# Linear attention with a mixture of experts on one core: key path ahead of the queries, ε of the keys as a column, and a VectorE add that waits for GpSimd's sums

## The reference

```python
def softmax_kernel(x, proj, is_query):            # per head, x: [.., n, 16]
    xp = einsum('bhnd,md->bhnm', x * norm, proj)
    diag = sum(square(x), -1) * 0.5 * norm * norm
    stab = max(xp, -1) if is_query else max(xp, (-1, -2))
    return ratio * (exp(xp - diag - stab) + EPS_K)
qp, kp = softmax_kernel(q, proj, True), softmax_kernel(k, proj, False)
k_sum = sum(kp, axis=2)
denom = einsum('bhnm,bhm->bhn', qp, k_sum)
ctx = einsum('bhnm,bhnd->bhmd', kp, v)
out = einsum('bhnm,bhmd->bhnd', qp, ctx) / denom[..., None]
x = layer_norm(video + out @ Wo.T + bo); x = layer_norm(x + relu(x @ W1.T + b1) @ W2.T + b2)
...
# experts: scores = softmax(xf @ gate_w.T); top 512 tokens of each expert; two products with gelu; scatter-add
```

## Time and profile before

| | |
|---|---|
| median of 3 runs | 785.98 us (785.49 to 787.17) |
| the profiled execution | 786.12 us |
| its span, first to last instruction | 784.4 us |
| granted TensorE clock, mean | 0.977 |
| PE, PEld busy | 93%, 76% |
| DVE, ACT, POOL busy | 79%, 60%, 48% |
| one turn of the steady loop | 58.1 us |
| end of turn 7 on PE | at 465.6 us |

### The profile page before, as it was taken

The page is one execution under the profiler, slowest core; times in us unless marked ns, Lnnn a source line. Parts: engine busy times, 40 slices in busy tenths (PEclk is TensorE's granted clock), DMA queues, the critical chain, the costliest instruction groups (busy, mean ns, idle before and its releaser), DMA issues. The chain is left out here.

```text
span 784.4 us, 16225 instructions
## 1 busy us (share of the span) xinstructions
PE 728.6 (93%) x6009; PEld 597.0 (76%) x6009; DVE 619.0 (79%) x1304; ACT 469.6 (60%) x749; POOL 375.3 (48%) x358
## 2 busy tenths in 40 slices
PE   8999999999999999999999979968999999999950
PEld 7867768778778778778778758857888889998850
DVE  5976678888888888888888797888768767778683
ACT  4656747867867867867868834463245544455470
POOL 4364317527527527527617613511347556544563
PEclk9999999999999999999999999999999999999985
DMA  8100010011011011011011011250336664446593
GB/s 252 33 2 2 1 54 2 28 54 57 28 53 54 27 53 54 27 53 54 27 54 29 29 55 54 60 193 2 124 134 163 160 165 112 107 148 168 138 266 112
DMA packets 51184, 62.60 MB, mean 80 GB/s; under 512 B 9408, under 2 KB 44992, under 8 KB 51136
## 3 DMA queue, kind: packets, MB, share of 16 engines
q1 hardware_dynamic: 44016, 49.74, 19.3%
q0 software_dynamic: 6864, 12.19, 7.9%
q10 hardware_dynamic: 256, 0.03, 0.0%
HBM read 40.85 MB, written 21.10 MB: 79 GB/s over the span
## 5 line engine op out<-in xcount | busy, mean ns | idle before, releaser
L2181 PE MATMUL pF<-w,h 128*128 128x256 f32 x448 | 109.8, 386 | 0.0
L2181 PEld LDWEIGHTS pF<-w,h 128*128 128x128 f32 x448 | 80.7, 190 | 17.6 <-issue 8.6
L1139 POOL DMA_INDIRECT kp<-row_scratch,idx_g x32 | 43.3, 1353 | 76.5 <-DVE idx_g L1851 53.5
L904 ACT ACTIVATE h<-pX,b1cur 128x512 f32<-128x512 f32 x64 | 43.9, 689 | 56.4 <-DVE b1cur L1954 41.8
L2636 PE MATMUL pX<-w_lo,h_hi 128*128 128x256 f32 x256 | 73.9, 289 | 0.8 <-issue 0.8
L2636 PE MATMUL pX<-w_hi,h_lo 128*128 128x256 f32 x256 | 72.4, 283 | 0.0
L2636 PE MATMUL pX<-w_hi,h_hi 128*128 128x256 f32 x256 | 72.4, 283 | 0.0
L993 POOL TENSOR_SCALAR ve<-mv 128x4 f32<-128x4 f32 x36 | 8.5, 237 | 133.2 <-DVE mv L1216 132.3
L1147 POOL DMA_INDIRECT acc_scratch<-qp,idx_s x28 | 55.5, 1982 | 21.5 <-DVE qp L1891 16.6
L1912 DVE TENSOR_TENSOR h_lo<-h,h_hi 128x512 fp32r<-128x512 f32 x64 | 42.5, 690 | 22.9 <-ACT h_hi L896 22.2
L1321 DVE RECIPROCAL den<-den 128x512 f32<-128x512 f32 x14 | 46.9, 3348 | 7.9 <-ACT den L551 7.9
(11 more groups left out here) (435 smaller groups left out, 2165.6 us busy)
## 6 DMA issues: line engine op xcount, KB each, us to landing
kp<-fc1T SPq DMA_DIRECT2D x8, 1024.0 KB
w<-fc2T SPq DMA_DIRECT2D x8, 1024.0 KB
xin<-video SPq DMA_DIRECT2D x7, 512.0 KB, 3.5
x<-video SPq DMA_DIRECT2D x7, 512.0 KB, 4.5
out<-x SPq DMA_DIRECT2D x7, 512.0 KB, 3.0
acc_scratch<-xf SPq DMA_DIRECT2D x7, 512.0 KB, 2.9
row_scratch<-y SPq DMA_DIRECT2D x7, 512.0 KB, 3.0
kp<-acc_scratch SPq DMA_DIRECT2D x4, 512.0 KB, 5.8
```

Of the source, the lines that this page charges most:

```text
L904: nc.scalar.activation(h[:, n, :], pM[n % M_SLOTS], ACT.Gelu_apprx_tanh, bias=b1cur[:, n:n + 1]).then_inc(he_ready, 1)
L1139: pool.indirect_dma_start(xg[:, g, :], None, row_d, bass.IndirectOffsetOnAxis(ap=idx_g[:, g:g + 1], axis=0)).then_inc(first_rows[g] if isi ...
L2181: ins = nc.tensor.matmul(pF[m][:, half * D:(half + 1) * D], h[:, k, tok(2 * m + half)], w2[:, k, :], start=(k == 0), stop=(k == FC - 1))
```

## The change

1. **ε of the keys.** `eps_k` goes. The key tiles lie with a pitch of 130 instead of 128 columns in a wider tile whose columns 128 and 129 hold ε; `context` reads 129 columns, so its last column is ε times the sum of the values, which `cs_copy(i, 0)` copies to `vsum` and adds as a bias; `cs_copy(i, 1)` adds 512 ε. The first turn's extra matmuls with ε, in `context` and `sums_of_keys`, and GpSimd's two adds for them go too.
2. **TensorE's order** in a turn: `key_features(0)` ahead of `values`; `turn_kmax` behind `hidden(2)` instead of `hidden(5)`; `context` ahead of `features_turned(0)` and without the product between them; `sums_of_keys`, `features_turned(1)` and `turn_context` one behind the other; 16 products of `ff_out` behind `all_heads`, where 10 stood. `spread_kmax` stands alone and reads 128 rows (the rows beyond 16 are zeros).
3. **VectorE's order:** `k_max` 0 and 1 ahead of `x2T_lo`; `q_max` 0 and 1 behind `k_top`; `rest_of_squares` behind `k_sub` 1; `residual` behind `ln1_stats` and `scores`, and it waits for `ksum_ready`.
4. **GpSimd's order:** the sums wait for all four `k_sub`; the add of `bo_b` to `xn` (`biased_rows`) waits for `obias_ready` and stands behind the sums.
5. **ScalarE's order:** `exp_k` 0 and 1 between the last `relu`; `z_norm` behind `exp_k`; `normed_rows` last. SyncE stores the scores of batch u one turn later.

The core of the diff:

```diff
@@ ScalarE, GpSimd @@
-                nc.scalar.activation(cs[:, n, :], pA[n][:, 0:G * P], ACT.Copy).then_inc(cs_ready, 1)
+                if n:
+                    nc.scalar.activation(cs[:, 1, :], pA[1][:, 0:G * P], ACT.Identity, bias=epsn_c[:, 0:1]).then_inc(cs_ready, 1)
+                else:
+                    wide = pA[0][:, 0:G * PW].rearrange("p (g x) -> p g x", x=PW)
+                    nc.scalar.activation(vsum[:].unsqueeze(2), wide[:, :, P:P + 1], ACT.Copy).then_inc(vsum_ready, 1)
+                    act.wait_ge(vsum_ready, i + 1)
+                    for g in range(G):
+                        ins = nc.scalar.activation(cs[:, 0, g * P:(g + 1) * P], wide[:, g, 0:P], ACT.Identity, bias=vsum[:, g:g + 1])
+                    ins.then_inc(cs_ready, 1)
...
-            def eps_k(i, t):
-                act.wait_ge(ke_ready, (i - 1) * TT + t + 1)
-                nc.scalar.activation(kp[:, t, :], kp[:, t, :], ACT.Identity, bias=epsk_c[:, 0:1]).then_inc(kp_ready, 1)
...
+                    pool.wait_ge(ks_ready, (i + 1) * TT)
+                    for t in range(1, TT):
                         pool.wait_ge(kp_ready, i * TT + t + 1)
...
+                if not is_first(i):
+                    pool.wait_ge(obias_ready, i + 1)
+                    biased_rows()
@@ VectorE @@
-                    q_max(i, 0)
-                    q_max(i, 1)
-                    k_top(i, sa)
-                    rest_of_squares(i)
-                    dve.wait_ge(dg_ready, (i + 1) * 2)
-                    k_shift(i)
-                    k_sub(i, 0)
-                    k_sub(i, 1)
-                    q_max(i, 2)
...
+                k_top(i, sa)
+                q_max(i, 0)
+                q_max(i, 1)
+                dve.wait_ge(dg_ready, (i + 1) * 2)
+                k_shift(i)
+                k_sub(i, 0)
+                k_sub(i, 1)
+                rest_of_squares(i)
+                q_max(i, 2)
...
+                if u is not None:
+                    dve.wait_ge(ksum_ready, (i + 1) * (TT - 1))
+                    residual(u, su)
@@ TensorE @@
-                steps = [(v[:, t], kp[:, t]) for t in range(TT)] + ([(vsum[:, 0:D], None)] if is_first(i) else [])
...
+                                ins = nc.tensor.matmul(s[32 * q:32 * q + 32, g * PW:g * PW + P + 1], v[:, t, 32 * pair:32 * pair + 32],
+                                                       kpe[:, t, place_of(pair), 0:P + 1], start=(t == 0), stop=(t == TT - 1),
+                                                       tile_position=(0, 32 * q))
...
+                hidden(2)
+                turn_kmax()
+                hidden(3)
+                hidden(4)
+                spread_kmax()
+                hidden(5)
+                features(i, J_XQ + 1, qT, 1)
+                hidden(6)
+                hidden(7)
+                ff_out(2)
+                turn_tops()
+                ff_out(6)
+                context()
+                features_turned(0)
+                ff_out(4)
+                sums_of_keys()
+                features_turned(1)
+                turn_context()
+                ff_out(4)
+                all_heads()
+                ff_out(5)
```

More of the change, by code:

```diff
@@ L736, in body @@
+                if not is_ahead(i):
                     squares(i, 0)
                     squares(i, 1)
[L738 to L766, removed]
+                key_rows(1)
+                relu(f, 0)
+                relu(f, 1)
@@ new lines, in body @@
+                q_squares(i)
+                for n in range(2, 6):
+                    relu(f, n)
+                exp_k(i, 0)
+                relu(f, 6)
+                exp_k(i, 1)
+                relu(f, 7)
+                q_tops(i)
+                exp_k(i, 2)
+                exp_k(i, 3)
+                if ut:
+                    for t in range(TT):
+                        z_norm(u, t)
+                cs_copy(i, 0)
+                exp_q(i, 0)
+                cs_copy(i, 1)
+                exp_q(i, 1)
@@ L2172, in hidden, with ff_out @@
                     by_halves(slot_f(f, J_H + n), w1_hi, w1_lo, x2T_hi, x2T_lo, n).then_inc(f_ready, 1)
-                def ff_out(m, half, k0=0, k1=FC):
-                    if half == 0:
-                        slot_f(f, J_Y + m)
-                    for k in range(k0, k1):
+                products = [(m, half, k) for m in range(2) for half in range(2) for k in range(FC)]
+                def ff_out(count):
+                    for m, half, k in products[:count]:
+                        if half == k == 0:
+                            slot_f(f, J_Y + m)
                         if m == half == 0:
@@ L2182, in ff_out @@
                                                start=(k == 0), stop=(k == FC - 1))
-                    if half == 1 and k1 == FC:
-                        ins.then_inc(f_ready, 1)
+                        if half == 1 and k == FC - 1:
+                            ins.then_inc(f_ready, 1)
+                    del products[:count]
                 def by_heads(j, w_, g):
@@ L2437, in body @@
-                if att:
-                    features(i, J_XQ + 1, qT, 1)
-                    spread_kmax()
-                if ff:
-                    hidden(7)
-                if ff:
-                    ff_out(0, 0)
-                    ff_out(0, 1, 0, 2)
-                if att:
-                    turn_tops()
-                if ff:
-                    ff_out(0, 1, 2, FC)
-                if att:
-                    features_turned(0)
-                if ff:
-                    ff_out(1, 0, 0, 1)
@@ L2453, in body @@
[L2453 to L2467 removed]
+                key_features(1)
@@ L2472, in body @@
                         turn_tokens(pXall[:, 2 + c, :], xf, c).then_inc(u_ready, 1)
[L2473 to L2474 removed]
+                ff_out(3)
                 if gt_:
```

247 lines of the change are left out of this document (92 added, 155 removed).

## The result

The changed kernel takes 789.63 us (median of 6, 787.73 to 791.23) against 785.49 us for the kernel before: ratio 1.0048, 95% interval 1.0028 to 1.0067. It is slower, by about what was forecast (790.0), but the trace shows that terms of the sum were wrong and cancelled in part. The profiled execution of the changed kernel took 787.73 us and was the fastest of the six.

A forecast was written before the change was run, and what follows sets the result against it. PE's stream plus any wait on PE was taken to bound the kernel. A full turn costs −0.6 + 0.6 + 1.0 = +1.0; with turns 0, 1 and 7 the sum is +4.2, giving 790.0 us, range 779 to 794.

The forecast's parts named there:

- PE's own stream: PE's work in a steady turn, without waits, falls by about 0.6 us, from 58.1 to 57.5.
- First wait: PE at turn_tops waits 0.6 us a turn: DVE's chain from spread_kmax takes 6.94 us against PE's 6.46.
- Second wait: PE at sums_of_keys waits 1.0 us more a turn: subtractions and POOL's three sums make 9.9 us against PE's 8.9.
- Residual, no cost to PE: Residual behind POOL's sums takes 1.23 us instead of 3.39, hidden by PE's work; without that cover, up to 0.5 a turn.
- Turn 0, −0.9: Four groups of ε products of 0.22 us go from a chain leading to the heads: −0.9 us.
- Turn 1, +1.0: k_max ahead of x2T_lo +0.9, both waits +1.6, waits at and behind attention_out gone −1.2, borders −0.3: together +1.0 us.
- Turn 7, −0.9: Heads come earlier in PE's stream, and DVE's reciprocal chain behind them moves along, except for 0.4: −0.9 us.
- The sum: Turn 0 −0.9, turn 1 +1.0, five full turns +5.0, turn 7 −0.9: +4.2 us, giving 790.0 us.
- the waits don't form: Rival: neither wait at turn_tops nor sums_of_keys appears, only PE's stream counts, −7.0 us or 779.0; chance 0.27, in full or larger part.
- one wait only: Rival: only one of the waits at turn_tops and sums_of_keys costs time, 784 to 787 us; chance 0.10.
- POOL holds VectorE elsewhere: Rival: POOL's root for z or small scores products hold VectorE or the sums, 0.9 us a turn, about 795 us; chance 0.08.
- What would show it: Both waits each turn, steady turn 59.1 us, residual 1.23; wrong if a turn is under 58 or PE's waits under 5 us.

The follow-up runs named there:

- e3: Changed kernel with one more ff_out product ahead of turn_tops and one ahead of sums_of_keys, two fewer behind all_heads; 784.94 us, 0.9975 of the kernel before.
- e10: Changed kernel with rest_of_squares moved behind k_sub 3 instead of ahead of q_max 2; 788.72 us, 1.0023 of the kernel before.
- e12: e6 with one more ff_out product ahead of sums_of_keys and one more ahead of turn_x, both from behind turn_x; 780.13 us, 0.9918 of the kernel before.
- e8: Kernel before with only part 1 of the change (pitch of 130, no eps_k, bias of the copies), old orders; 797.87 us, 1.0142 of the kernel before.
- e9: e8 plus the change's two waits: GpSimd's sums for all four subtractions, the residual, behind the statistics, for the sums; 802.40 us, 1.0184 of the kernel before.
- e6: Changed kernel with the edits of e3 and e4, and in turn 1 k_max(1) behind x2T_lo again; 782.16 us, 0.9941 of the kernel before.
- e4: Changed kernel with VectorE's copy of the gates behind turn 7 put after the third reciprocal and product pair; 787.44 us, 1.0010 of the kernel before.
- e1: Changed kernel run again with nothing altered; 790.37 us, 1.0050 of the kernel before.
- e2: Changed kernel with VectorE's residual no longer waiting for GpSimd's key sums; 794.72 us, 1.0101 of the kernel before.
- e11: e10 plus the gates copy moved as in e4 and, in turn 1, the second k_max behind x2T_lo; 786.46 us, 0.9990 of the kernel before.
- e7: Changed kernel without GpSimd's wait for all four subtractions before its sums; 809.18 us, 1.0288 of the kernel before.

## Why the prediction was right, and where it was not

*The bound.* Right: PE's stream plus waits on PE. e3, e10 and e12 change only orders, and the turn became shorter by the waits that went.

*PE's own stream, −0.6.* Measured −0.80 (58.08 to 57.28, and 57.29 in e12). `attention_out` went from 3.40 to 3.02 (forecast −0.3); 0.4 is left for the borders, where I had 0.3.

*First wait, 0.6.* It is there, 0.40. The chain from `spread_kmax` took 6.94 as summed; PE's pieces took 6.59 for 6.46, and the step from DVE to PE 0.05 for 0.15.

*Second wait, 1.0.* It is there, 0.68. The mis-sized term is the pace of the sums: 2.40 for the first and 2.2 for each behind it, 6.9 us for the 7.35 that I summed from the 4.90 for two in turn 1. That row was undisturbed: VectorE ran nothing beside its two sums (2.39 and 2.37) but the last 0.04 us of one operation. In the changed kernel the same pair takes 4.51, and in e8 and e9, which have the old orders and the new layout of the key tiles, an undisturbed sum in place takes 2.18 to 2.20 too. So the gain came with the layout with its pitch of 130; I had taken the layout to leave the sums as they were. Why it helps is not shown. PE's pieces, which I wrote as 8.9 though they sum to 8.84, took 8.72.

So a full turn costs +0.28 and not +1.0 (+0.50 in turn 2), five of them +1.6 and not +5.0.

*Residual, no cost to PE.* Right in the changed order; e9 shows the cover that I named taken away, at 2.6 us a turn (58.08 to 60.64) where I had written 0.5. The part that I had priced, the masked context, is 0.7 of it. I had not priced the other 1.8: in the old order ScalarE's denominators stand behind `xf`, which needs the statistics behind the residual.

*Turn 0, −0.9.* Measured −1.13. Of this 0.91 lies behind the first `features_turned`, as forecast; the other 0.22 lies ahead of it, where from 32 to 40 us the granted clock was 0.79 and 0.78 in the profile before and 1.00 in the changed one. *Turn 1, +1.0.* Measured +0.38; its waits are the same smaller ones (0.47 and 0.65), and the `k_max` costs 0.65 for the 0.9 I gave it (e6). The wait of 1.03 at `attention_out` is gone, as forecast.

*Turn 7, −0.9.* This is the step that failed: +1.09. I had moved VectorE's reciprocal chain with the heads and not seen that it holds a copy which waits for the gates, which the change puts later. e4 puts that at 2.2 us, and −0.9 + 2.2 = +1.3 is near what was measured.

*The sum.* +4.2 forecast; the marks of the two profiled executions give +1.95, the two spans +1.6, the medians +4.1 and, in e1, +3.45. So that 790.0 came so near is luck twice. Within the turns, five were over by 3.4, turn 1 by 0.6 and turn 0 by 0.2, and turn 7 was under by 2.0, which leaves a forecast of +4.2 for a measured +1.95. The medians then hold about 2 us that the sum had no term for and that the two profiled executions do not show. Behind the last mark, with the same code, the profile of the kernel before has 316.1 us, that of the changed kernel 316.2 and those of the e-runs 316.4 to 318.3. Two stretches with a lower clock make most of this: 1.4 us in the first 8 us behind the mark, where the clock is low for 3.4 us (e1, e4 and e9), and 2.0 us between 81 and 97 us behind it (e2, e3, e6, e8, e10, e11 and e12). At the second place the clock is low for 3.5 us in the two first profiles and for 10.1 in those seven. A window of PE there in e10, then in the changed kernel, 94 us behind the mark in both:

```profile
562.93:564.93 2.00, 2.00 (x9) 0.50 0.60 172
```

```profile
563.78:565.78 2.00, 2.00 (x13) 1.00 0.60 168
```

e8 and e9, with the orders of the kernel before, have such stretches too. The mean granted clock over the executions of e1 was 0.974 for the changed kernel and 0.975 for the kernel before, so whether the changed kernel meets them more often stays open.

*The rivals.* That the waits don't form fell, as they are in every turn; one wait only fell too. That POOL holds VectorE elsewhere did not happen in the changed kernel's steady turns: `sdiag` takes 0.22 us, in turn 4 with the root for z running beside it from the start, and the small products of `scores` take 0.18 each. Only in turn 7 one of these, beside a sum, took 2.17, with VectorE idle behind it. But the mechanism is what the two waits keep away, as e7, e8 and e2 show. I had looked for it where the change might bring it in, and not for what the change guards.

*What would show it.* The waits and the residual as written; a turn of 58.36 meets "not under 58". The two waits sum to 7.9 us over the seven turns (5.6 by the brackets), over the 5 that I had set.

## What to carry to other kernels

Removing work from one engine moves the start of the next one's work, and that start can fall on an operation that it holds: the four ε adds were never on the path, and taking them away alone cost 12 us. In e7 the lower clock that followed each of five such waits cost nearly as much again as the wait. Price the removal by what then starts earlier and what runs at that moment on the engine that shares a resource with it; a wait that looks like cost may be the guard. And where a chain at the program's end has its own written order, follow every instruction in it to its input, also those that belong to another batch.

## What the runs showed of the hardware

A VectorE copy that casts 64 elements a partition takes 0.19 us alone, and 1.65 and 2.17 us when it is issued 0.75 and 0.23 us after a GpSimd add of two SBUF tiles has begun: it ends as that add ends. VectorE operations with two SBUF inputs and GpSimd's adds hold each other in either order (residual 2.72 and two sums 5.31 in e2; `rest_of_squares` first, then a sum of 3.22 in e10). The statistics (1.40 for four in both kernels) ran beside sums at their usual length, and `q_max`, which reads PSUM, took 1.23 and 1.21 us beside GpSimd's add of a bias to x in turn 4 of the kernel before, and takes 1.20 to 1.22 throughout the changed one.

The Trainium skill, SBUF — State Buffer, section Who interferes with whom, says that a copy or cast can enter a mode that takes the port pair shared with GpSimd, that whoever issues first has it for the whole instruction, and that the order of issue decides who is blocked. The trace agrees: in e7 and e8 the GpSimd add was first and the copy ended with it, and in e10, where VectorE was first, the sum was the longer one.

A GpSimd add in place of 1024 columns (key sum plus key tile) took 2.36 to 2.39 us, with no VectorE operation of two SBUF inputs beside it, when the tile lay in one piece (the kernel before) and 2.17 to 2.20 when it lay as eight pieces of 128 at a pitch of 130 (the changed kernel, e7 to e10).

The granted clock of TensorE fell to 1.2 GHz for part of a stretch of some us, and not in each execution at the same place. In turn 0 the same code took 40.0 us in eight profiles, 40.13 in e10 (0.76 and 0.81 from 32 to 40 us), 41.15 in e11, where the clock was low for part of 28 to 40 us, and 41.56 in e6, where it was low for part of 12 to 20 us. In e7 PE stood still for 2.2 to 2.3 us ahead of `turn_tops` in each turn; the clock fell behind this in turns 3 to 7 (0.64 over the next 4.8 us in turn 4) and not in turns 1 and 2.
